# Layer-1 attention: one shared power for two normalisations, rows fetched four batches ahead, six indirect transfers in a row

## The reference, cut to what matters

```python
x2 = x + tanh(g_ffn[0]) * (y_shared + p0 * y0 + p1 * y1)        # y rows chosen per token, from the experts of layer 0
q  = layernorm(x2) @ Wq + bq;  k = ctx @ Wk + bk;  v = ctx @ Wv + bv
x3 = x2 + tanh(g_xattn[1]) * softmax(q @ k.T) @ v               # no scale
z  = layernorm(x3)                                              # input of router and experts of layer 1
gates = softmax((z @ w_red) @ normalised(wg).T);  idx = argmax(gates)
```

## Time and profile before

| | us |
|---|---|
| median of 3 runs (1225.4 to 1228.27) | 1225.59 |
| the profiled execution | 1229.47 |
| its span in the trace | 1227.7 |
| PE busy over the span | 1061.5 (86%) |
| DVE busy | 715.3 (58%) |
| ACT busy | 598.3 (49%) |
| POOL busy | 448.7 (37%) |

### The profile page before, as it was taken

How to read it: one execution, slowest core, us unless ns; L and a number is a source line. 1 busy time by engine, 2 the same in 40 slices (tenths; PEclk the granted TensorE clock), 3 DMA queues, 4 the chain that set the end, 5 groups by cost and what they waited for, 6 DMA issues and landing times. The chain is left out here.

```text
span 1227.7 us, 30253 instructions
## 1 busy us (share of the span) xinstructions
PE 1061.5 (86%) x8055; PEld 817.9 (67%) x8056; DVE 715.3 (58%) x2338; ACT 598.3 (49%) x1374; POOL 448.7 (37%) x581
## 2 busy tenths in 40 slices
PE   3999999999999971999999999957888887179996
PEld 2677777777777751777777777745676766146664
DVE  5567777777777654344444433334766665445664
ACT  3467666676666630444444444425565565123332
POOL 3345665666656523000000000015766772212222
PEclk9799999999999965999999999977988988589999
DMA  4123211222111212354444433335633330444441
GB/s 134 32 62 94 73 62 57 68 85 80 60 57 45 72 42 90 91 125 128 125 127 128 128 95 85 83 95 182 197 117 104 125 106 37 120 97 106 111 111 50
DMA packets 153538, 116.26 MB, mean 95 GB/s; under 512 B 87696, under 2 KB 141250, under 8 KB 153219
## 3 DMA queue, kind: packets, MB, share of 16 engines
q1 hardware_dynamic: 112082, 57.46, 17.6%
q10 hardware_dynamic: 30816, 28.63, 7.8%
q0 software_dynamic: 10576, 29.41, 7.1%
HBM read 51.82 MB, written 45.92 MB: 80 GB/s over the span
## 5 line engine op out<-in xcount | busy, mean ns | idle before, releaser
L1483 PE MATMUL e_first<-w_high,e_z_cols 128*128 x824 | 174.3, 314 | 21.3 <-DMA e_z_cols<-z_rows 20.9
L1582 DVE SCALAR_TENSOR_TENSOR e_hidden<-e_first,e_act_out 128x352 f32<-128x352 f32 x103 | 54.0, 525 | 164.8 <-ACT e_act_out L1528 164.8
L1214 PE MATMUL a_out<-a_v_ones,a_probs 128*128 128x65 f32 x1024 | 142.2, 283 | 0.0
L1214 PEld LDWEIGHTS a_out<-a_v_ones,a_probs 128*128 128x128 f32 x1024 | 128.4, 197 | 14.9 <-issue 14.9
L1700 POOL IOTA a_first_numbers<- 128x2 int32 x1 | 0.1, 127 | 339.8 <-POOLq L70 339.8
L547 POOL DMA_INDIRECT z_rows<-r_z_halves,r_slot_idx x96 | 96.3, 1003 | 74.4 <-DVEq L529 39.9
L1483 PEld LDWEIGHTS e_first<-w_high,e_z_cols 128*128 128x128 f16 x824 | 80.7, 98 | 56.8 <-issue 21.8
L1528 ACT ACTIVATE e_act_out<-e_first 128x352 f32<-128x352 f32 x103 | 47.8, 464 | 135.8 <-PE e_first L1483 135.1
L856 ACT ACTIVATE a_probs<-a_scores,a_latent_bias,a_k_scales 128x256 f32<-128x256 f32 x128 | 65.4, 561 | 99.3 <-PE a_scores L1200 63.8
L1587 DVE TENSOR_TENSOR e_hidden_low<-e_hidden_cols,e_hidden_high 128x384 f16<-128x384 f32 (+1 forms) x142 | 84.2, 593 | 48.4 <-ACT e_hidden_high L1537 48.4
L1483 PE MATMUL e_first<-w_low,e_z_cols 128*128 x412 | 95.6, 314 | 0.0
(11 more groups left out here) (342 smaller groups left out, 2843.6 us busy)
## 6 DMA issues: line engine op xcount, KB each, us to landing
y_rows<-e_y_rows ACTq DMA_DIRECT2D x103, 128.0 KB, 1.7
w_stage<-in_v ACTq DMA_DIRECT2D x64, 128.0 KB, 2.3
w_stage_first<-in_w SPq DMA_DIRECT2D x18, 352.0 KB, 2.9
a_ctx_in<-in_ctx SPq DMA_DIRECT2D x32, 192.0 KB, 2.8
e_token_rows<-z_rows ACTq DMA_DIRECT2D x39, 129.0 KB, 2.3
residual<-in_x SPq DMA_DIRECT2D x16, 256.0 KB, 2.9
z_rows<-r_z_halves SPq DMA_DIRECT2D x16, 256.0 KB, 2.2
a_y_shared<-y_rows SPq DMA_DIRECT2D x16, 256.0 KB, 2.9
```

The costliest lines, as they stand in the source:

```text
L1214: ins = pe.matmul(O[t][:, h * (D + 1):(h + 1) * (D + 1)], pm[x][:, jt, t * P:(t + 1) * P], va[p][:, jt, h, :], start=i + x == 0, stop=i + ...
L1483: ins = pe.matmul(GU[p][f][:, 0:F], x[z][:, k, :], w[:, ds(off, F)], start=(k == 0 and x is xh and w is wh), stop=(k == KC - 1 and x is xl))
L1582: v.scalar_tensor_tensor(hs[p][:], GU[p][1][:, 0:F], 1.0 / WSCALE, act_out[:], ALU.mult, ALU.mult).then_inc(hidden_done, 1)
```

## The change

It does five things, all in attention 1 except for the tile `minus_one`, which goes from the constants with its memset:

1. DVE adds the epsilon and negates the mean itself (two operations of 128x2 for each layer norm) and writes them to the halves of two shared tiles of 128x4: columns 0 and 1 belong to the layer norm of x2, columns 2 and 3 to that of x3 (z).
2. POOL's `norms(n)` takes the place of `rt.pool_rstd(n-1)` and `rstd(n+2)`: one power and one product over all four columns (two columns where only one of the batches exists), behind a wait for both statistics, `s1_stats` of batch n+2 and `rt.stats_ready` of batch n-1.
3. ACT's `act_z(n-1)` and `pre_norm(n+2)` both wait for that product (`norm_ready`).
4. POOL fetches batch n+4 behind `norms(n)` and in front of the scatter of n-2; DVE's `slots` run for batch n+4 and behind `x2_mean_var(n+2)`.
5. DVE waits for each of its aggregations before it reads them, and before it writes the shared tiles it waits for the power that read them last.

```diff
     def pool_rstd(self, pool, n):
-        ch = Chain(pool, self.pool_step, n * (6 - 2 * self.K))
+        ch = Chain(pool, self.pool_step, n * 2)
...
-        if self.K == 1:
-            ch.link(pool.tensor_tensor(self.shift[:], self.mv[:, :, 0], self.g["minus1"][:], ALU.mult))
-            ch.link(pool.tensor_tensor(self.shift[:], self.shift[:], self.rstd[:], ALU.mult))
     def vector_stats(self, v, n, x):
...
         if self.K == 1:
-            v.wait_ge(self.z_high, count(n))
-            v.sem_inc(self.g["carried_v"], 1)
+            for t in range(T):
+                ch.mark(v.bn_aggr(self.mv[:, t, :], self.st[:, t, :]))
+            ch.wait()
+            return
...
+        var, nmean, rstd, shift = (sb(f"norm_{x}", [P, 2 * T]) for x in ("variance", "minus_mean", "rstd", "shift"))
...
-                def rstd(m):
-                    ch = Chain(pool, p1, m * P1)
-                    pool.wait_ge(s1_stats, m + 1)
-                    ch.link(pool.tensor_tensor(r1[:], mv[:, :, 1], g["epst"][:, 0:T], ALU.add))
-                    ch.link(pool.tensor_tensor(r1[:], r1[:], g["mhalf"][:, 0:T], ALU.pow))
-                    ch.link(pool.tensor_tensor(shift[:], mv[:, :, 0], g["minus1"][:], ALU.mult))
-                    ch.link(pool.tensor_tensor(shift[:], shift[:], r1[:], ALU.mult))
-                    pool.sem_inc(s1_rstd, 1)
+                def norms(n):
+                    ch = Chain(pool, p1, n + 2)
+                    lo, hi = 0 if within(n + 2, B) else T, 2 * T if within(n - 1, B) else T
+                    if lo == 0:
+                        pool.wait_ge(s1_stats, n + 3)
+                        pool.wait_ge(s1_norm, count(n + 2))
+                    if hi > T:
+                        pool.wait_ge(rt.stats_ready, n)
+                        pool.wait_ge(rt.z_ready, count(n - 1))
+                    ch.link(pool.tensor_tensor(rstd[:, lo:hi], var[:, lo:hi], g["mhalf"][:, lo:hi], ALU.pow))
+                    pool.tensor_tensor(shift[:, lo:hi], nmean[:, lo:hi], rstd[:, lo:hi], ALU.mult).then_inc(norm_ready, 1)
...
                 def step(n, q):
-                    if within(n - 1, B):
-                        rt.pool_rstd(pool, n - 1)
-                    if within(n + 3, B):
-                        fetch(n + 3, 1 - q)
...
-                    if within(n + 2, B):
-                        rstd(n + 2)
+                    if within(n + 2, B) or within(n - 1, B):
+                        norms(n)
...
+                    if within(n + 4, B):
+                        fetch(n + 4, q)
                     if within(n - 2, B):
                         rt.pool_scatter(pool, n - 2, q)
...
                 def pre_norm(m):
-                    act.wait_ge(s1_rstd, m + 1)
+                    act.wait_ge(norm_ready, m + 1)
...
                     if tail:
-                        rt.act_z(act, n - 1, XRTile(g["XR"], n - 1))
+                        act.wait_ge(norm_ready, n + 3)
+                        rt.act_z(act, n - 1, XRTile(g["XR"], n - 1), rstd[:, T:2 * T], shift[:, T:2 * T])
...
                 def x2_mean_var(m):
                     ch = chains["x2"]
-                    v.wait_ge(s1_norm, count(m))
                     ch.wait()
                     v.sem_inc(g["carried_v"], 1)
                     for t in range(T):
-                        ins = v.bn_aggr(mv[:, t, :], st[:, t, :])
-                    ins.then_inc(s1_stats, 1)
+                        ch.mark(v.bn_aggr(mv[:, t, :], st[:, t, :]))
+                    ch.wait()
+                    v.wait_ge(norm_ready, count(m))
+                    v.sem_inc(g["carried_v"], 1)
+                    v.tensor_scalar(var[:, 0:T], mv[:, :, 1], EPS, None, ALU.add)
+                    v.tensor_scalar(nmean[:, 0:T], mv[:, :, 0], -1.0, None, ALU.mult).then_inc(s1_stats, 1)
...
                     rt.vector_stats(v, m, XRTile(g["XR"], m))
+                    v.wait_ge(norm_ready, m + 3)
+                    v.sem_inc(g["carried_v"], 1)
+                    v.tensor_scalar(var[:, T:2 * T], rt.mv[:, :, 1], EPS, None, ALU.add)
+                    v.tensor_scalar(nmean[:, T:2 * T], rt.mv[:, :, 0], -1.0, None, ALU.mult).then_inc(rt.stats_ready, 1)
...
                     if core:
                         maxima(n)
-                    if within(n + 3, B):
-                        slots(n + 3, 1 - q)
...
                     if within(n + 2, B):
                         x2_mean_var(n + 2)
+                    if within(n + 4, B):
+                        slots(n + 4, q)
```

More of the change, by code:

```diff
@@ L100, in program @@
         g["epst"] = sb("eps_tile", [P, 4])
-        g["minus1"] = sb("minus_one", [P, T])
         g["gate"] = sb("tanh_gates", [P, 4])
@@ L158, in _ @@
                 v.memset(g["epst"][:], EPS)
-                v.memset(g["minus1"][:], -1.0)
                 v.memset(g["padding"][:], 0.0)
@@ L311, in __init__ @@
         self.st = sb("stats", [P, T, 6])
-        self.rstd, self.shift = sb("rstd", [P, T]), sb("shift", [P, T])
+        if K == 2:
+            self.rstd = sb("rstd", [P, T])
         self.L = sb("logits", [P, T, E])
@@ L361, in pool_rstd @@
         ch.link(pool.tensor_tensor(self.rstd[:], self.rstd[:], self.g["mhalf"][:, 0:T], ALU.pow))
-        if self.K == 1:
-            ch.link(pool.tensor_tensor(self.shift[:], self.mv[:, :, 0], self.g["minus1"][:], ALU.mult))
-            ch.link(pool.tensor_tensor(self.shift[:], self.shift[:], self.rstd[:], ALU.mult))
         pool.sem_inc(self.rstd_ready, 1)
     def vector_stats(self, v, n, x):
-        ch = Chain(v, self.stat_step, n * T)
+        ch = Chain(v, self.stat_step, n * T * (3 - self.K))
         v.sem_inc(self.g["carried_v"], 1)
@@ L390, in vector_z, with act_z @@
         ins.then_inc(self.z_ready, 1)
-    def act_z(self, act, n, x):
-        act.wait_ge(self.rstd_ready, n + 1)
+    def act_z(self, act, n, x, rstd, shift):
         act.wait_ge(self.z_turned, count(n))
@@ L399, in act_z @@
         for t in range(T):
-            ins = act.activation(self.z[:, t, :], x[:, t, :], ACT.Identity, bias=self.shift[:, t:t + 1], scale=self.rstd[:, t:t + 1])
+            ins = act.activation(self.z[:, t, :], x[:, t, :], ACT.Identity, bias=shift[:, t:t + 1], scale=rstd[:, t:t + 1])
         ins.then_inc(self.z_ready, 1)
@@ L1632, in phase_attn1 @@
         cin = [sb(f"ctx_in{p}", [P, T, DC]) for p in range(2)]
-        st, mv, r1, shift = sb("stats", [P, T, 6]), sb("mean_var", [P, T, 2]), sb("rstd", [P, T]), sb("shift", [P, T])
+        st, mv = sb("stats", [P, T, 6]), sb("mean_var", [P, T, 2])
+        var, nmean, rstd, shift = (sb(f"norm_{x}", [P, 2 * T]) for x in ("variance", "minus_mean", "rstd", "shift"))
         xn = sb("x_norm", [P, T, C])
@@ L1651, in phase_attn1 @@
         s1_ctx_turned, s1_ctx_cols = sem("s1_ctx_turned"), sem("s1_ctx_cols")
+        norm_ready = sem("norm_ready")
         proj_ready, freed_act, v_tokens, ones_ready = sem("proj_ready"), sem("proj_freed_act"), sem("v_tokens"), sem("ones_ready")
@@ L1655, in phase_attn1 @@
         d1, d2, p1 = sem("dve_step1"), sem("dve_step2"), sem("pool_step1")
-        D1, D2, P1 = 7, 4, 4
+        D1, D2, P1 = 7 + T, 4, 1
         loads = [(bq[:], a["bq1"]), (wq[:], a["wq1"].rearrange("(k p) f -> p k f", p=P)),
@@ L1707, in fetch @@
                             gather(pool, idx[p], k, t, g["y0"], yk[p][:, k, t, :], gathered[p])
-                def rstd(m):
-                    ch = Chain(pool, p1, m * P1)
-                    pool.wait_ge(s1_stats, m + 1)
-                    ch.link(pool.tensor_tensor(r1[:], mv[:, :, 1], g["epst"][:, 0:T], ALU.add))
-                    ch.link(pool.tensor_tensor(r1[:], r1[:], g["mhalf"][:, 0:T], ALU.pow))
-                    ch.link(pool.tensor_tensor(shift[:], mv[:, :, 0], g["minus1"][:], ALU.mult))
-                    ch.link(pool.tensor_tensor(shift[:], shift[:], r1[:], ALU.mult))
-                    pool.sem_inc(s1_rstd, 1)
-                    assert ch.n == P1
+                def norms(n):
[9 more added lines that the diff above has]
+                    pool.tensor_tensor(shift[:, lo:hi], nmean[:, lo:hi], rstd[:, lo:hi], ALU.mult).then_inc(norm_ready, 1)
                 def step(n, q):
-                    if within(n - 1, B):
-                        rt.pool_rstd(pool, n - 1)
-                    if within(n + 3, B):
-                        fetch(n + 3, 1 - q)
                     if isinstance(n, int) and n == -2:
@@ L1752, in pre_norm @@
                     for t in range(T):
-                        ins = act.activation(xn[:, t, :], x[:, t, :], ACT.Identity, bias=shift[:, t:t + 1], scale=r1[:, t:t + 1])
+                        ins = act.activation(xn[:, t, :], x[:, t, :], ACT.Identity, bias=shift[:, t:t + 1], scale=rstd[:, t:t + 1])
                     ins.then_inc(s1_norm, 1)
@@ L1916, in step @@
                         maxima(n)
-                    if within(n + 3, B):
-                        slots(n + 3, 1 - q)
                     if within(n - 2, B):
```

(4 more changed lines are left out.)

## The result

The changed kernel takes 1279.61 us (median of 4 runs, 1275.16 to 1289.8) against 1226.93 for the kernel before on the same chip: a ratio of 1.0436, with an interval of 1.0365 to 1.0508. Its profiled run took 1275.16, span 1273.5, 45.8 above the span before. The phases ahead of the layer-1 attention happened to be 4.7 us shorter in that profile (the attention's first GpSimd instruction stands at 812.59, before at 817.32), so the attention alone is some 50 us longer. That start also moves between runs in which nothing ahead of it was edited: in the traces of this document it lies between 811 and 820 us, so the phases ahead add some microseconds of scatter to every comparison of medians.

A forecast was written before the change was run, and what follows sets the result against it. GpSimd's occupation was taken to bound the kernel at 13.08 us a step; a new circle would make it 17.4: 3.6 + 12 x (17.4 - 13.08) - 1.6 = 53.8 onto 1225.59, so 1279 us, range 1252 to 1300.

The forecast's parts named there:

- GpSimd's occupation as the period before: Layer-1 attention before the change: GpSimd's own work, 12.97 us, sets the step of 13.08 us, although TensorE is busier.
- It never rests: GpSimd in one step before the change: no waiting for other engines, 12.97 us of occupation.
- What goes off GpSimd: GpSimd's step in the attention: eight small operations become two, 9.90 us instead of 12.97, 3.1 us of room.
- The circle: Shared power, z, probability columns, products, x3, next step's maxima, choice, x2 work, back to the power: 15.6 us a step.
- The clock: TensorE rests some 5 us before z's turn; turn and products at half clock add 2.14 us: 17.4 in most steps.
- Start and tail: Attention's ends: first shared power 3.6 us late in step 1; steps 14 to 16 save 0.53 each, -1.6.
- The sum: Whole kernel: start, twelve longer steps and tail add 53.8 us to the median 1225.59, giving 1279.
- The six in a row buy nothing: GpSimd's four gathers and two scatters behind the power end near t0 + 9 (t0: shift's end), then some 5 us waiting.
- the wait for y at the start: VectorE in step 1 stood 2.61 us for y; fetching four batches ahead removes that wait.
- The faster rival: GpSimd's occupation stays the period until TensorE bounds at 11.4 us a step: 1202 us, chance 0.04.

The follow-up runs named there:

- more_before: The kernel before with two more gathers behind each fetch, into a tile that nothing reads: 1258.18 us, ratio 1.0243.
- more_after: The changed kernel with two more gathers behind each fetch, into a tile that nothing reads: 1279.74 us, ratio 1.0445.
- warm10: The changed kernel with 10 filler matmuls a step on TensorE in front of z's turn, results unread: 1265.33 us, ratio 1.0326.
- double_power: The changed kernel with the shared power computed twice in a row, writing the same values: 1295.72 us, ratio 1.0556.
- split: The changed kernel with the shared power split into two 128x2 powers, one behind the other, all else kept: 1219.12 us, ratio 0.9936.
- three_ahead: The changed kernel, power still shared, with batch n+3 fetched in front of the power and slot copies in front of the choice: 1296.04 us, ratio 1.0559.

## Why the prediction was right

The forecast was 1279, and 1279.61 was measured. Its steps, against the trace of the changed kernel:

- **GpSimd's occupation as the period before.** Shown by `more_before`, where 2.04 of 2.54 added us appear in each step, and by `more_after` that it no longer is. "It never rests" was read from one step and is too strong for the others: in the step ahead of it GpSimd stood 1.79 us in front of the scatter at 957.33, released by the slot index, where it stands 1.06 in the earlier trace rows without a wait.
- **What goes off GpSimd.** Forecast 3.1 us of room; the power took 1.04 as counted, the product 0.20, the lower of its two bounds. From the product to the first gather there are 0.67 us, not 1.02 as in the earlier trace rows, so the room was a little more, and it bought nothing in this order.
- **The circle.** From the shift: z 0.22 (forecast 0.27), the end of the probability columns 2.51 (2.56), x3 to maxima 3.30 (3.22), maxima to logits 0.61 (0.61), logits to aggregation 4.39 (4.41), aggregation to the next shift 2.29 (2.20). All links but TensorE's were full-clock rows of before and came out within 0.1 in this turn. Over the twelve steps the links from x3 on make 10.22 us, forecast 10.43; most of the difference is x3 to maxima, 2.99 in the mean (it alternates, mostly between 2.9 and 3.3) and 3.22 forecast. `warm10` has the whole circle at full clock at 15.26, so this term, 15.6, was 0.3 too long. `double_power`, `warm10` and `split` show that it is this circle.
- **The clock.** The rest came as forecast (5.19 us, forecast some 5), and the clock was 0.50 behind it in the turn shown. But it had gone down within the rest already (mean 0.89 in 992 to 993, 0.50 in 993 to 994; the rest is 990.97 to 996.16) and came back within the products, which took 3.15 us, not 3.62: x3 starts 6.78 behind the shift, 1.63 more than at full clock, where the forecast had 2.14 in most steps. Over the twelve steps x3 starts 6.90 us behind the shift in the mean, 5.10 in `warm10`: 1.80 more. The whole step shows 17.12 - 15.26 = 1.86, forecast 1.8. So the size was right, for a reason that was not quite the forecast's: not full price in most steps, but part of it in every one.
- **Start and tail.** Measured from the attention's first instruction, step 1's shift is at 43.13, before at 39.83: 3.3 late (forecast 3.6). From step 13's shift to the end of the last scatter 47.5 us, before 47.9: -0.4, forecast -1.6. The operations saved did count: from the end of a scatter to the end of the shift behind it stand 1.03 us in steps 14 to 16, before 1.58, three times 0.55 as forecast. What the forecast left out is the clock in the tail: behind step 13's shift the scatter came 9.01 us later, before 7.06, with products of 3.49 us against 1.89; against it, before had low-clock products of 3.62 us near 1039 where the changed kernel's of that step took 2.85.
- **The sum.** 3.3 + 12 x 4.04 - 0.4 = 51.4, forecast 53.8. Put onto 1225.59 this is 1277; the measured median is 2.6 higher. So the mechanism was right, but the agreement of 1279 with 1279.61 to within a microsecond is luck: the circle was 0.3 a step too long, the tail 1.2 too short, and the median's scatter made up for the rest. The runs of the changed kernel differ more than before's, with the mean granted clock of the whole run: 0.917 in that of 1275.16, 0.904 in that of 1289.8.
- **"The six in a row buy nothing".** True of the comparison with the kernel before, but too short: `three_ahead` shows that with the power shared the later fetch saves 16 us, of which 2.4 are the wait for y at the start that the forecast named.

The faster rival (1202) needed the two statistics to be ready together. The experiments reached that time in the opposite way, with two powers.

## What to carry to other kernels

Before two stages of a software pipeline share one small operation, write down when each of its inputs is ready, who stands behind each consumer in its engine's program, and whether the path comes back to the operation; then count that circle from rows. Occupation saved on the bounding engine is worth nothing beyond the point where such a circle becomes longer than it. To know whether an engine's occupation is the bound, give it a known piece of extra work in both kernels: gathers of 2.54 us a step lengthened the step by 2.04 us in one (29.6 us in all) and by nothing in the other.

## What the hardware showed that I had not expected

- In the turn shown the granted clock was at 0.50 from the rest on and came back some 3.5 us behind the start of z's turn (0.70 in 999 to 1000, 1.00 in 1000 to 1001). In the turn of the earlier trace rows it fell only behind the rest, and all of the 6.4 us until it came back lay over matmuls. Ten filler matmuls a step raised the whole run's clock from 0.917 to 0.952.
- From a tensor operation to the first indirect transfer GpSimd had a gap of 0.67 to 0.68 us here and 1.03 in the earlier trace rows. There a separate semaphore instruction stood between them; no run shows that this is the reason.
- A 128x4 product took 0.19 to 0.20 us, no more than a 128x2 one, while the power took 1.04 against 0.72.
- An fp32 matmul of 128x256 took some 0.44 us at full clock (20 of them 8.9 us), as two records of the profile.
